# Moving the loads of the input rows from SyncE's queue to ScalarE's in the last graph stage of a two-part GNN

## What is computed

```python
x = _layernorm(x + _L0_gnn_ref(x, W, b, gamma, beta, edge_index), axis=-1)
x = _layernorm(x + _L1_gnn_ref(x, src, dst, edge_attr_20, edge_weight, edge_attr_3, ...), axis=-1)
```

## Time and profile before

| what | value |
|---|---|
| median of 3 runs | 1652.86 us (1648.44 to 1658.84) |
| the profiled execution's own time | 1654.69 us |
| its span in the profile | 1653.0 us (1.69 us lie around it) |
| mean granted clock of TensorE | 0.889 of full speed |
| busy share of the span | PE 80%, DVE 68%, ACT 55%, POOL 54% |
| DMA | 330.64 MB, 200 GB/s over the span |
| `finish_gcn` in 1129 to 1365 us | PE 102.3, DVE 173.5, ACT 145.5, POOL 79.4 us busy of 236; mean DMA share 0.85, 313 GB/s |

### The profile page before, as it was taken

The page is one execution under the profiler, slowest core; times in us unless marked ns, Lnnn a source line. Parts: engine busy times, 40 slices in busy tenths (PEclk is TensorE's granted clock), DMA queues, the critical chain, the costliest instruction groups (busy, mean ns, idle before and its releaser), DMA issues. The chain is left out here.

```text
span 1653.0 us, 24539 instructions
## 1 busy us (share of the span) xinstructions
PE 1322.7 (80%) x7509; PEld 1122.2 (68%) x7509; DVE 1117.2 (68%) x3189; ACT 902.3 (55%) x1789; POOL 897.5 (54%) x788
## 2 busy tenths in 40 slices
PE   3775799999999799999987999994554435999981
PEld 3664687888877688888876888883443324777760
DVE  7558466556566576767846877885787765677772
ACT  3760344333334576767664766643666663566663
POOL 5772667777774667878734243220333343356655
PEclk8887799999999899999998999996666667999995
DMA  2001888778777667677655665637888863255544
GB/s 65 3 2 34 297 277 278 246 256 264 262 234 260 218 224 252 236 256 264 238 189 164 212 220 186 218 112 237 330 331 329 321 270 79 61 110 131 132 99 106
DMA packets 133078, 330.64 MB, mean 200 GB/s; under 512 B 34420, under 2 KB 66828, under 8 KB 130132
## 3 DMA queue, kind: packets, MB, share of 16 engines
q1 hardware_dynamic: 80372, 185.94, 32.1%
q0 software_dynamic: 52576, 143.13, 28.7%
HBM read 166.39 MB, written 167.16 MB: 202 GB/s over the span
## 5 line engine op out<-in xcount | busy, mean ns | idle before, releaser
L1050 PE MATMUL ps_b<-yhi,whi 128*128 128x492 f32 (+1 forms) x960 | 398.1, 415 | 20.8 <-ACT aggT L942 16.3
L1050 PE MATMUL ps_b<-ylo,whi 128*128 128x492 f32 (+1 forms) x960 | 379.1, 395 | 0.0
L1050 PE MATMUL ps_b<-yhi,wlo 128*128 128x492 f32 (+1 forms) x960 | 379.0, 395 | 0.0
L942 ACT COPY aggT<-ps_b 128x492 f32<-128x492 f32 (+1 forms) x240 | 137.6, 574 | 314.2 <-PE ps_b L1050 314.0
L860 DVE BATCH_NORM_STATS2 stat<-aggT 128x6 f32<-128x492 f32 (+1 forms) x240 | 161.9, 677 | 151.4 <-ACT aggT L942 148.3
L702 POOL DMA_INDIRECT rows<-rows_out,node_at x160 | 185.7, 1161 | 110.6 <-ACT rows_out L948 64.7
L1050 PEld LDWEIGHTS ps_b<-yhi,whi 128*128 128x128 f32 x960 | 185.7, 193 | 52.1 <-ACT aggT L942 16.6
L1050 PEld LDWEIGHTS ps_b<-yhi,wlo 128*128 128x128 f32 x960 | 184.5, 192 | 38.5
L1050 PEld LDWEIGHTS ps_b<-ylo,whi 128*128 128x128 f32 x960 | 185.8, 193 | 30.3 <-issue 0.5
L1178 POOL DMA_INDIRECT out<-fin_out,node_at x80 | 79.4, 992 | 185.8 <-DVE fin_out L1247 97.2
L709 POOL TENSOR_TENSOR X<-X,own_row 128x1016 f32<-128x1016 f32 x40 | 96.3, 2410 | 131.6 <-ACT X L926 131.3
(11 more groups left out here) (407 smaller groups left out, 2941.9 us busy)
## 6 DMA issues: line engine op xcount, KB each, us to landing
z<-aggT SPq DMA_DIRECT2D x30, 1016.0 KB, 5.1
z<-aggT SPq DMA_DIRECT2D x30, 984.0 KB, 6.0
x_rows<-R SPq DMA_DIRECT2D x80, 256.0 KB, 3.9
fin_xr<-x_rows SPq DMA_DIRECT2D x20, 1024.0 KB, 9.3
X<-z SPq DMA_DIRECT2D x20, 1016.0 KB
X<-z SPq DMA_DIRECT2D x20, 984.0 KB
x<-fin_x SPq DMA_DIRECT2D x10, 1024.0 KB, 10.1
fin_X<-z SPq DMA_DIRECT2D x10, 1016.0 KB, 14.2
```

The lines of the kernel that those rows point to most:

```text
L942: nc.scalar.copy(f.aggT[t % 2][:, j, 0:cols(t)], f.ps_b[j % 2][:, 0:cols(t)]).then_inc(x["copied"], 1)
L1050: o = nc.tensor.matmul(f.ps_b[j % 2][:, 0:n], w[:, c, j * P:(j + 1) * P], y[g % 2][:, c, 0:n], start=(c == 0 and i == 0), stop=(c == C - 1 ...
```

## The change

SP no longer issues xr(b) for b from 3 to 19. ACT issues them: in its turn t, after `prep.scalar_turn` and before the first root, it issues xr(t+3), behind the same wait (blocks up to t-1 normed). The first three xr (L1145) stay with SP. All else keeps its place; SP's store and SP's loads of X keep their waits.

```diff
             for b in range(3, NB):
                 sp.wait_ge(x["turned"], 4 * (b - 2))
                 sp.dma_start(f.X[b % 3][:, :, 0:cols(b)], z_in[b, :, :, 0:cols(b)]).then_inc(z_got[b % 3], 16)
-                ge(sp, x["normed"], 4 * (b - 3))
-                sp.dma_start(f.xr[b % 4][:], x_rows[b]).then_inc(x_in[b % 4], 16)
                 if m.edges(b - 4):
                     keep(b - 4)
                 if b == 4:
...
             def body(t):
                 prep.scalar_turn(act, Turn(0, t, NB - 1, 4))
+                if 3 <= t + 3 < NB:
+                    b = t + 3
+                    ge(act, x["normed"], 4 * (b - 3))
+                    act.dma_start(f.xr[b % 4][:], x_rows[b]).then_inc(x_in[b % 4], 16)
                 if runs(t + 1):
```

## The result

The changed kernel takes 1659.74 us in the median of 20 runs (1651.00 to 1669.28), the kernel before 1652.67 us on the same chip (1648.44 to 1659.05, 20 runs). The ratio is 1.0042, with a 95% interval of 1.0027 to 1.0057: slower by 0.4%, some 7 us. The profiled execution took 1661.78 us; its span is 1659.7 us against 1653.0.

A forecast was written before the change was run, and what follows sets the result against it. The last graph stage was taken as a loop set by the bytes ahead of odd X and by ACT behind it. Terms +15.4 and -5.0 gave +10.4 us, a median of 1663 us, with an 8 in 10 range of 1645 to 1672.

The forecast's parts named there:

- xr(even): Head of each period, even xr issued by ACT instead of SP: same bytes ahead of odd X, so 0.
- xr(odd): Loop of the last graph stage: odd xr shares the engines with odd X, +2.2 us per period, 7 times, +15.4 us.
- The start: Start of the stage: X(5) no longer held behind xr(4), -6.1, +0.8 for X(3), +0.3 for an issue, sum -5.0 us.
- Seventeen issues on ACT: ACT's turns: time for issuing the xr loads, 5.4 us, hidden by its waits for odd X, so 0.
- xr landing later: DVE's adds: xr(10) sharing with the store lands at most 2.5 us later, still in time, so 0.
- One line for all: Rival, chance 0.22: requests served in issue order whichever engine issues; loop keeps its period, only the start gains, 1648 us.
- The start brings nothing: Rival, chance 0.14: SP is held, X(5) issued after about 1166 us; only the loop's loss stands, 1670 us.
- SP's queue first: Rival, chance 0.06: odd X overtakes both xr and lands 2.5 us earlier each period, 1629 us.
- It does nothing that counts: Rival, chance 0.08: X(5)'s gain is eaten by X(3), and the period stays, 1653 us.

## Why the prediction was right, and where it was off

The forecast was 1663 us, +0.6%, and no measurable change the likeliest; 1659.74 us and +0.4% came. The sum was +10.4 us; the medians say +7.1 (4.5 to 9.4 by the interval), the stage of the profiled executions +4.0. Beside the run with the even loads alone, 8.5 us shorter at head 8, the odd loads cost 12.5 us in the stage and all the rest gains 8.5; I had +15.4 and -5.0. The mechanism held, with each half some 3 us too high. That the number came nearer than the stage did is luck: some 3 us of the difference lie outside the stage, and nothing in the forecast stands for them.

*xr(even), put at 0.* This term failed: "the engines are full from soon after on and the bytes ahead of X(11) are the same". The bytes are, but they are not moved as late as before. The run with the even loads alone measured -0.8 us per period from head 2 on. The engines are far from full in the first 2 us behind the head (66 GB/s), and more moves there when ACT issues xr(even); SP's issue of odd X comes 0.4 us earlier besides. I had noticed the 0.4 and let it vanish in "full from soon after on".

*xr(odd), +2.2 per period.* Mechanism and size held: 2.4 alone, near the upper bound of 2.5 as I chose, with odd X landing at 17.3 us where I expected about 17. "x 7" was too many for the two halves together. Period by period the changed kernel is longer than the run with the even loads alone by 0.1, 0.4, 3.1, 2.7, 2.5, 2.5 and 1.0 us: four full charges, three small ones. In the period with no loss xr(9) was issued 10.2 us behind the head (1202.65 to 1212.89), in the one after 8.8 us (1223.75 to 1232.51); in 1216 to 1217.86, before X(9) was there, ACT's queue had moved only 0.27 MB. Up to the landing of the X that is waited for, ACT's queue had moved 1.00, 0.88, 1.05 and 0.99 of xr(odd)'s 1.05 MB in the four periods with a full charge, and 0.73, 0.27 and 0.64 MB in the first, second and last. So the charge goes with how much of xr(odd) moves before odd X is through; the first period (0.73 MB, 0.1 us) does not fit this alone. That it also explains the wider spread of the changed kernel's runs (18.3 us against 10.6) is argued, not shown.

*The start, -5.0.* The first head came 6.1 us earlier, and xr(4) alone gave 5.5 in the stage, 4.5 in the time. X(5) left at 1159.92, which is 29.35 us into the stage, the 1158.43 that I had read from before (29.33), and without any wait of ACT. X(3) was read 0.90 us later in the stage, near the 0.8 charged, though xr(3) left 2.6 us earlier than I had it (17.08 us into the stage, not 19.70). But neither this charge nor the 0.3 for the issue lasted: before, the wait for X(5) began 41.94 us into the stage (1171.04); now X(5) is read 41.94 us into it (1172.51). So the start was worth the full 6.1. What I did not see is that the first period gives part of it back, +2.7 us, and does so with the even loads alone as well (+2.6). X(7) is issued into engines that are still busy: in the first 3.6 us behind head 1 they moved 285 GB/s, where before moved 66 in the first 2 us behind its head 1:

```profile
1178.39:1182.00 3.61, 0.00 (x0) 0.00 (x0) 3.40 (x15) 2.96 (x5) 0.94 (x1) 0.97 0.96 285
```

With xr(4) alone they are nearly as busy there (249 GB/s in the first 3.6 us), and only 1.0 came back. So the busy engines alone do not explain the 2.7; the rest goes with the other even loads, and its cause stays open.

*Seventeen issues on ACT, 0.* Right: 0.33 to 0.39 us each, beside ACT's work or ahead of a wait, and the kernel with all 17 and the odd ones late is as fast as the one with eight of them (0.9945 and 0.9946).

*xr landing later, 0.* Right: in 1195 to 1300 us the even ones land 6.8 to 7.2 us after their issue (before 6.2 to 6.6), and no wait of DVE for xr appears among the waits.

The rivals. "One line for all" falls, since who issues decides: with the even loads on ACT, the same odd loads give 0.9946 when SP issues them and 1.0042 when ACT does. "The start brings nothing" falls with X(5). "SP's queue first" falls with the queues' rows; yet its 1629 us is about what the kernels take in which odd X really goes first (1629.18 and 1626.68). "It does nothing that counts" falls too, though by little: the interval leaves out 1, and is much finer than the 1% that I thought a measurement could tell.

The Trainium skill (same page, section "Issuing engines are not separate DMA queues") holds that issuing from several engines saves only the time of the issues. In this case it does not hold: eight loads moved to ACT gain 0.5%, nine others cost 1.4%, and the rows show that the issuing engine decides which transfers share and which follow each other.

## What to carry to other kernels

Moving a transfer to a second queue took it out of line here: it helped what had stood behind it and hurt what was still to come in the old queue while it moved. So ask for each transfer which late one it will share the engines with. Before spreading loads over queues, look for a load whose buffer is free but which stands behind another's wait: taking that wait from in front of it was worth 1.3 to 1.5% here, while the new queue with the wait in place lost 0.4%. A gain at the head of a loop shows first; follow it period by period, since the next period may take some back.

## What the runs showed that was not expected

A load issued by ACT while SP's queue was backlogged began to move late: xr(11), issued at 1232.51, had 0.09 of its 1.05 MB through by 1237, while SP's moved 0.94 MB from 1233 on; from then on it had as many packets as SP's. Why it takes these 4 us is open. And with two queues more moves from nearly idle engines: 147 to 164 against 61 to 106 GB/s in the first 2 us behind a head. Part of that may be that the store is issued 0.4 us earlier.
